# Five seams between stages of a two-layer graph network: barriers and clearing of semaphores taken out, signals for the buffers put in

## The reference

```
xn = layernorm(x)
x  = x + gated graph network(xn, edges) + linear attention(xn)        # layer 0, softmax-like feature map
x  = x + mixture of 8 experts, top 2 (layernorm(x))
xn = layernorm(x)
x  = x + (edge-weighted 1024x1024 matrix applied to xn, + bias) + linear attention(xn)   # layer 1
x  = x + w_down(silu(w_gate xn') * (w_up xn')),  xn' = layernorm(x), integer weights / 127
```

## Time and profile before

| | us |
|---|---|
| median of three runs | 2345.37 |
| lowest and highest | 2345.21, 2346.77 |
| span of the profiled execution | 2343.6 |
| TensorE busy | 2181.0 (93%) |
| VectorE busy | 1513.5 (65%) |
| ScalarE busy | 1015.1 (43%) |
| GpSimd busy | 252.9 (11%) |
| barriers of line 74 | 11 |

### The profile page before, as it was taken

One profiled execution on the slowest core, in us unless ns is written; L12 is line 12 of the kernel. 1 busy time (PEld: TensorE's weight loads), 2 busy tenths in 40 slices (PEclk: granted clock), 3 DMA queues, 4 the chain that ended last, 5 costly groups with the idle time before them and its releaser, 6 DMA issues. The chain is left out here.

```text
span 2343.6 us, 29202 instructions
## 1 busy us (share of the span) xinstructions
PE 2181.0 (93%) x10522; PEld 1799.2 (77%) x10522; DVE 1513.5 (65%) x2245; ACT 1015.1 (43%) x1515; POOL 252.9 (11%) x253
## 2 busy tenths in 40 slices
PE   7999999978968999976999999968999999989998
PEld 4778888867857778775888888856778888878886
DVE  8745474668858788866999999966733333345422
ACT  4134243338725544425888888851022122121120
POOL 0067774000010000020000000011000000000000
PEclk9999999988988999967999999989999999999999
DMA  5431231114448535164555555136420120134224
GB/s 189 143 112 36 50 83 24 65 58 151 146 152 315 215 158 225 46 239 154 182 203 183 209 183 182 63 110 212 133 76 34 48 81 25 63 103 153 75 90 149
DMA packets 114121, 299.89 MB, mean 128 GB/s; under 512 B 18802, under 2 KB 42218, under 8 KB 113974
## 3 DMA queue, kind: packets, MB, share of 16 engines
q1 hardware_dynamic: 103094, 276.52, 33.9%
q0 software_dynamic: 10880, 21.48, 3.3%
HBM read 295.24 MB, written 124.16 MB: 179 GB/s over the span
## 5 line engine op out<-in xcount | busy, mean ns | idle before, releaser
L2717 DVE TENSOR_TENSOR ex_wl<-exlast,ex_wh 128x1024 fp32r<-128x1024 f32 x216 | 252.7, 1220 | 9.1 <-ACT ex_wh L2784 8.5
L2784 ACT ACTIVATE ex_wh<-exlast 128x1024 fp32r<-128x1024 f32 x216 | 217.9, 1059 | 17.3 <-PE ex_pu L2740 8.2
L1267 POOL DMA_INDIRECT scratch_slots<-packed x160 | 196.5, 1228 | 56.7 <-issue 56.7
L324 PE MATMUL ps<-kept,xh 128*128 128x512 f32 (+2 forms) x480 | 160.1, 420 | 7.2 <-DVE xl L3008 5.5
L2117 PE MATMUL gl_bank<-gl_gh,gl_al 125*125 125x512 f32 x385 | 153.5, 399 | 9.7 <-DVE gl_al L2332 9.7
L1564 PE MATMUL ps<-kept,xl 128*128 128x512 f32 (+1 forms) x640 | 159.2, 391 | 0.0
L1566 PE MATMUL ps<-kept,xh 128*128 128x512 f32 (+1 forms) x640 | 158.3, 389 | 0.0
L1570 PE MATMUL ps<-kept,xh 128*128 128x512 f32 (+1 forms) x640 | 158.2, 389 | 0.0
L2119 PE MATMUL gl_bank<-gl_gh,gl_ah 125*125 125x512 f32 x385 | 152.8, 397 | 0.0
L2118 PE MATMUL gl_bank<-gl_gl,gl_ah 125*125 125x512 f32 x385 | 152.6, 396 | 0.0
L1566 PEld LDWEIGHTS ps<-kept,xh 128*128 128x128 f32 (+1 forms) x640 | 118.5, 185 | 26.9
(11 more groups left out here) (513 smaller groups left out, 4885.6 us busy)
## 6 DMA issues: line engine op xcount, KB each, us to landing
exlast<-in_experts SPq DMA_DIRECT2D x216, 512.0 KB
exfirst<-in_experts SPq DMA_DIRECT2D x112, 512.0 KB, 6.2
scratch_seats<-raw SPq DMA_DIRECT2D x95, 512.0 KB
raw<-in_qkv SPq DMA_DIRECT2D x48, 512.0 KB, 5.2
xr<-scratch_res SPq DMA_DIRECT2D x27, 512.0 KB, 4.3
xr<-scratch_seats SPq DMA_DIRECT2D x27, 512.0 KB, 3.7
scratch_res<-xr SPq DMA_DIRECT2D x25, 512.0 KB, 3.9
raw<-in_wo SPq DMA_DIRECT2D x16, 512.0 KB, 4.8
```

Of the source, the lines that this page charges most:

```text
L324: i = e.matmul(o, a, b[:, cut], start=first and n == 0, stop=final and n == 2)
L1267: e.indirect_dma_start(dram["slot_rows"], bass.IndirectOffsetOnAxis(idx[:, k:k + 1].bitcast(U32), 0), pay[:, k, :], None).then_inc(scat.se ...
L2717: return e.tensor_tensor(wl[:, n % RING], raw[unit[1]], wh[:, n % RING].bitcast(F32), ALU.subtract)
L2784: e.activation(wh[:, n % RING], raw[unit[1]], ACT.Copy).then_inc(high.sem)
```

## The change

`Phase` gets a flag `wall`. With `wall=False` (stages `em`, `o0`, `ex`, `se`, `o1`) nothing at all is issued at the stage's end; the semaphores are kept in a common list `spent`. With `wall=True` (`m0`, `gb`, `gl`, `ro`, `m1`, `ff`) a barrier comes first, then the clearing of all of `spent`, then the second barrier. `block()` gives a `Stream` that puts each body straight into the engine's list, without a block of its own and its barrier; only `gb`, which branches, still opens a block (`branches()`), and so keeps the block's barrier too.

The seams without a barrier are `em` to `m0`, `o0` to `gb`, `ex` to `se`, `se` to `m1`, `o1` to `ff`.

```diff
-    def __init__(self, nc, tag):
+    spent = []
+    def __init__(self, nc, tag, wall=True):
...
         if a[0] is None:
-            self.nc.clear_and_free_semaphores(self.sems)
-            self.nc.all_engine_barrier()
+            self.spent += self.sems
+            if self.wall:
+                self.nc.all_engine_barrier()
+                self.nc.clear_and_free_semaphores(self.spent)
+                self.nc.all_engine_barrier()
+                self.spent.clear()
...
     def block(self):
+        return Stream(self.nc)
+
+    def branches(self):
         return self.ctx.enter_context(self.nc.Block())
```

Signals that now guard what is passed on. In `em` and `se` TensorE raises `slot_free` in its last chunk, when a slot of `kept` has been read for the last time, and `attention`'s first four `hi` wait for it; GpSimd in `attention` waits for VectorE's last addition of the stage before (`settled`); TensorE in `ff` waits for the last low part of the normalized input:

```diff
@@ sort_and_embed, TensorE
+                    elif c == TC - 1 and k % 2:
+                        y.then_inc(slot_free.sem)
@@ serve, TensorE
+                    if c == TC - 1 and k < SLOTS:
+                        m.then_inc(slot_free.sem)
@@ attention, GpSimd
         def _(e):
+            e.wait_ge(*settled.last())
             for a in range(2):
@@ attention, ScalarE, hi(u)
                 elif u[0] >= 2:
                     e.wait_ge(*kv_done[u[0] // 2 - 1, TC - 1])
+                else:
+                    e.wait_ge(*slots_free[kv_slot(u)])
                 e.activation(held(0, u), raw[:, nth[u] % SLOTS], ACT.Copy).then_inc(high.sem)
@@ gated_mlp, TensorE
         def _(e):
+            e.wait_ge(*normed_low.last())
```

More of the change, by code:

```diff
@@ L58, in last, with __init__, sync, gpsimd @@
         return self.sem, max(self.value.values())
+class Stream:
+    def __init__(self, nc):
+        self.nc = nc
+    def sync(self, f):
+        f(self.nc.sync)
+    def gpsimd(self, f):
+        f(self.nc.gpsimd)
+    def tensor(self, f):
+        f(self.nc.tensor)
+    def scalar(self, f):
+        f(self.nc.scalar)
+    def vector(self, f):
+        f(self.nc.vector)
 class Phase:
-    def __init__(self, nc, tag):
-        self.nc, self.tag, self.ctx, self.sems = nc, tag, ExitStack(), []
+    spent = []
+    def __init__(self, nc, tag, wall=True):
+        self.nc, self.tag, self.wall, self.ctx, self.sems = nc, tag, wall, ExitStack(), []
     def __enter__(self):
@@ L346, in sort_and_embed @@
     assert all(v * OVER >> SHIFT == v // TP for v in range(N)) and EP < P and EK < 256 and EP < 256 and EK % QC == 0
-    with Phase(nc, "em") as p:
+    with Phase(nc, "em", wall=False) as p:
         sb = p.sb
@@ L379, in sort_and_embed @@
         q_high, q_low, begun = (p.raises(n_, ["q"]) for n_ in ("q_high", "q_low", "begun"))
+        slot_free = p.raises("slot_free", range(3))
         xb, xn = flat(xb), room.take([P, 2, D], F32)
@@ L802, in sort_and_embed @@
         stored = x_out[0:2] + x1_out
-        p.hand_on(*ahead.loaded, *stored, begun)
-    return ahead, stored, begun
+        p.hand_on(*ahead.loaded, *stored, begun, slot_free, done, summed)
+    return ahead, stored, begun, [slot_free[s] for s in range(3)] + [done[TC - 1]], [slot_free, done], summed
 def project(nc, tag, at, xh, xl, w_dram, base, out, raw, first, more, at_stored, base_stored, then, then_scale, xr, kept, ps, ar):
     SLOTS, MADE, BEGUN = 4, 4, 4
-    with Phase(nc, tag) as p:
+    with Phase(nc, tag, wall=False) as p:
         C, U, HALVES = range(TC), range(KC), [slice(0, D // 2), slice(D // 2, D)]
@@ L970, in _ @@
             split(TC - 1)
-        p.hand_on(*ahead.loaded, *x_out, begun)
-    return ahead, x_out, begun
+        p.hand_on(*ahead.loaded, *x_out, begun, low)
+    return ahead, x_out, begun, low
 def project_and_count(nc, tag, at, w_dram, bias_dram, res, dram, c16, first, more, at_stored, xr, halves, ps, ox, ar0):
@@ L1298, in graph_overflow @@
         pw = [ctx.enter_context(nc.psum_tensor(f"gb_pw{i}", [P, 4, P], F32)) for i in range(4)]
-        block = p.block()
+        block = p.branches()
         def some(e):
@@ L1399, in _, with attention @@
                 e.tensor_copy(counted, cacc[:, 0:NBUCK * TP]).then_inc(counts.sem)
-def attention(nc, tag, xh, xl, at, w_dram, bq_dram, bkv_dram, softly, raw, first, then, xr, xr_free, kept, ps, begun, place, onto, beside=None, taken=(), room=None):
+def attention(nc, tag, xh, xl, at, w_dram, bq_dram, bkv_dram, softly, raw, first, then, xr, xr_free, kept, ps, begun, place, onto, slots_free, freed, settled, beside=None, taken=(), room=None):
     PAIRS, SLOTS, RING = KC, 4, 3
@@ L1408, in attention @@
     with Phase(nc, tag) as p:
-        p.take(*first.loaded, *taken, begun)
+        p.take(*first.loaded, *taken, *freed, begun, settled)
         J, C, T = range(PAIRS // 2), range(TC), range(NT)
@@ L2873, in serve @@
         spent, q_high, q_low, begun = (p.raises(n_, ["q"]) for n_ in ("spent", "q_high", "q_low", "begun"))
+        slot_free = p.raises("slot_free", range(SLOTS))
         warm = p.sb("warm", [P, 1])
@@ L3041, in _, with gated_mlp @@
                 evict(c)
-        p.hand_on(*ahead.loaded, *x_out, begun)
-    return ahead, x_out, begun
-def gated_mlp(nc, tag, xh, xl, up_dram, down_dram, hc, dtype, scale, res, out, raw, first, res_stored, xr, kept, ps, begun):
+        p.hand_on(*ahead.loaded, *x_out, begun, slot_free, added)
+    return ahead, x_out, begun, [slot_free[s] for s in range(SLOTS)], [slot_free], added
+def gated_mlp(nc, tag, xh, xl, up_dram, down_dram, hc, dtype, scale, res, out, raw, first, res_stored, xr, kept, ps, begun, normed_low):
     units = 2 * hc
@@ L3053, in gated_mlp @@
     with Phase(nc, tag) as p:
-        p.take(*first.loaded, *res_stored, begun)
+        p.take(*first.loaded, *res_stored, begun, normed_low)
         w = Weights(raw, kept, scale)
@@ L3230, in build @@
                     idx, packed = packed[0:EP, 4].bitcast(I32), flat(packed)
-                    ahead, x_stored, begun = sort_and_embed(nc, xh, xl, io["x"], io["w1"], io["b1"], x1, res, graph, idx,
+                    ahead, x_stored, begun, slots_free, freed, settled = sort_and_embed(nc, xh, xl, io["x"], io["w1"], io["b1"], x1, res, graph, idx,
                                                             pay, spill, raw, io["qkv0"], xr, kept, ps, Room(cnt[:]),
@@ L3235, in build @@
                         nc, "m0", xh, xl, at, io["qkv0"], io["bq0"], io["bkv0"], True, raw, ahead, io["wo0"], xr,
-                        x_stored, kept, ps, begun, place, (ar0[:], ox[:, 0], ox[:, 1], 2),
+                        x_stored, kept, ps, begun, place, (ar0[:], ox[:, 0], ox[:, 1], 2), slots_free, freed, settled,
                         lambda e, p: scatter(e, p, graph, idx, pay, 0, EK), x_stored, Room(cnt[:]))
@@ L3263, in build @@
                 place = [place[:, h] for h in range(2)]
-                ahead, res_stored, begun = serve(nc, "se", xh, xl, served, answer, share, graph["weights"], io["gnn_bias"],
+                ahead, res_stored, begun, slots_free, freed, settled = serve(nc, "se", xh, xl, served, answer, share, graph["weights"], io["gnn_bias"],
                                                  io["bo1"], res, raw, ahead, res_stored, io["qkv1"], xr, served_last, kept, ps,
@@ L3269, in build @@
                                                          ahead, io["wo1"], xr, res_stored, kept, ps, begun, place,
-                                                         (ar[:, 0], xh[:, :, tokens(0)], xl[:, :, tokens(0)], 4))
-                    ahead, res_stored, begun = project(nc, "o1", at, xh, xl, io["wo1"], res, res, raw.bitcast(I32), ahead, more,
+                                                         (ar[:, 0], xh[:, :, tokens(0)], xl[:, :, tokens(0)], 4),
+                                                         slots_free, freed, settled)
+                    ahead, res_stored, begun, normed_low = project(nc, "o1", at, xh, xl, io["wo1"], res, res, raw.bitcast(I32), ahead, more,
                                                        at_stored, res_stored, io["ffn_up"], SCALE, xr, kept, ps, ar)
             gated_mlp(nc, "ff", xh, xl, io["ffn_up"], io["ffn_down"], 3, I32, SCALE, res, io["out"],
-                      raw.bitcast(I32), ahead, res_stored, xr, kept, ps, begun)
+                      raw.bitcast(I32), ahead, res_stored, xr, kept, ps, begun, normed_low)
 def kernel(**a):
```

## The result

| | before | after |
|---|---|---|
| median, us | 2346.07 (6 runs) | 2340.86 (6 runs) |
| lowest to highest | 2345.21 to 2350.25 | 2338.32 to 2342.19 |
| span of the profiled execution | 2343.6 | 2339.2 |
| barriers after clearing | 11 | 6 |
| range clears | 73 | 40 |

The ratio is 0.9968, 95% interval 0.9958 to 0.9977: faster, by 0.23 to 0.42%. The medians of the table differ by 5.2 us (0.22%), just under that interval. I had forecast 14.3 us; the ratio makes it 7.5 of 2346, the two profiled executions 4.4. The new median, 2340.86, lies 0.9 us above the end of my range; beside a kernel before at 2345.4, from which I had worked, the ratio gives 2337.9, inside it. The head of the page answers to the earlier trace rows: the span is shorter and TensorE's busy time the same.

The account below looks back on a forecast made before the run. TensorE, busy 2181 of 2343.6 us, was taken to set the pace in most stages. Terms 4.1 + 2.3 - 0.3 + 1.5 + 3.1 + 2.1 + 1.5 = 14.3 gave span 2329.3, median 2331.1 us; range 2326 to 2340.

Parts of the forecast that it names:

- em to m0, 4.1 us: First seam: TensorE's 1.6 us barrier wait and 2.5 us wait for ScalarE both go; lower end 2.7 us.
- o0 to gb, 2.3 less 0.3: VectorE reaches the end of gb's block 2.3 us earlier; gb's own barriers cost about 0.3 us more.
- ex to se, +1.5 us: Serve's head: ScalarE's earlier start and the gather give 1.5 us, between 0.5 and 2.4.
- se to m1, 3.1 us: Same as the first seam: TensorE's waits of 2.0 and 1.1 us go.
- o1 to ff, 2.1 us: TensorE's barrier wait of 2.1 us goes, as its next group's weights are already in kept.
- The clearing, +1.5 us: At the walls, 33 ranges vanish and about 9 more go, each 0.17 us: 1.5 us gained, bounds -5.6 and +3.
- clearing only moves: Rival: the seams' range clears come back at the walls without merging; gain 7.2 us, time 2338.2; chance 0.12.
- fewer than 40: Sign in the profile after: fewer than 40 range clears are left.
- the 2 us that I had named as a sign of being wrong: Sign at the walls: the prediction is wrong if their clearing takes over 2 us each.
- The slow rival (instruction supply): Rival: without barriers TensorE waits for instructions, 4.0 us at each of five seams; 2351.1, slower; chance 0.06.
- the gains inside attention are lost: Rival: gains in m0 and m1 are lost before their wall; gain 7.1 us, median 2338.3; chance 0.09.
- The change does little: Rival: something just behind the barrier holds each seam; only o1 and gb barrier time saved; about 2347; chance 0.06.

Follow-up runs that it names:

- only_em: Kernel with walls everywhere but at the first seam, em to m0, against the kernel before; ratio 0.9982, span 2339.7.
- ex_wall: Changed kernel with the wall kept at the end of the experts stage (ex) only; ratio to the kernel before 0.9937, 2334.5 us against 2349.1.
- only_ex: Kernel with walls everywhere but at the seam from experts to serve (ex to se), against the kernel before; ratio 1.0024.
- gather_first: Changed kernel, with SyncE in serve waiting for both gathers of chunk 0 before loading weights of units 4 to 7 and rows of chunk 1; ratio 0.9962.
- bias_order: Changed kernel with attention's query bias loaded before the first weights and ScalarE waiting for it after four high parts, not two; ratio to the kernel before 0.9953.
- after_again: The changed kernel itself, unedited, run again beside the kernel before on the follow-ups' chip; ratio 0.9964, span 2337.3.
- after: The changed kernel as first measured against the kernel before; median 2340.86 us, ratio 0.9968, span 2339.2.

## Why the forecast was right in its sign and about twice the measured gain

- **em to m0, 4.1 us: right.** The lead grows by 4.4, and `only_em` has 3.9 us in its span. The bias landed later than I had it (negation at 131.87, not 130.1), which cost nothing: the margin of 1.6 us was there, and no wait is left.
- **o0 to gb, 2.3 less 0.3: right.** `gl` starts 5.5 us behind VectorE's last addition instead of 7.6; the lead grows by 2.2.
- **ex to se, +1.5 us: wrong, it was -5.1.** This is the step that failed. I had the two facts in hand: that the gather can't start before the store lands, and that the DMA engines are 90% busy behind it. I had even written that SyncE's loads now enter ahead of the gathers. I used all this only to shrink the gain, with a lower end of 0.5. What I left out is that an early queue next to one that can't move is harmful: SyncE's loads, which before were held until behind both gathers by ScalarE's late start (`low` of the first weights, itself after the barrier), now pass the second gather. `ex_wall`, `only_ex` and `gather_first` show it from three sides. And the 1.5 was too much even without the collision, where the seam gives 0.4. The Trainium skill states that the queues share the same 16 engines and interleave ("Trainium Kernel Development and Optimization", Key Constraints). These traces agree: the second gather could be used 11.2 us after its issue beside the loads and 5.5 us without them. The consequence here should have been a rival with a negative price, not a smaller gain.
- **se to m1, 3.1 us: 2.2.** The barrier's share came, the bank's wait stayed (1.1, then 1.3), because it hung on the bias's load: issued at 1720.56, negated at 1725.28, 4.7 us later. I had copied the answer of the first seam, where the load is issued 3.3 us before TensorE's first product and not 0.9 (126.68 and 130.00; 1720.56 and 1721.47). `bias_order` takes the wait away.
- **o1 to ff, 2.1 us: right** (2.3).
- **The clearing, +1.5 us: wrong in size.** That the 33 ranges vanish was right (73 became 40, so the rival "clearing only moves" falls). So forty are left, and my sign "fewer than 40" failed: that nine more would go was wrong. Six went, two at `m0`'s wall and four at `m1`'s, and six came, at `gb`, `gl` and `ff`. By the ranges in the two programs the cleared numbers now reach up to 223, and not to 166, with handed-on signals spread among them; that this makes the new gaps is my reading. And I took a range to cost the same whatever its length, while at `m0`'s wall 3 ranges take 1.3 us between the first start and the last (521.7 to 523.0), where 5 took 0.9 (525.9 to 526.8). Of the 1.3 us the long record itself is 0.57; another 0.6 lie between the starts of the second and the third clear, and nothing here explains them. I had expected every wall to gain; 0.9 us of lead went at this one. Added over the six walls, the distance from first to last clear grew from 6.1 us to 7.6: the term was a cost of about 1.5, not a gain of 1.5. The last wall, with 2.1, also passes the 2 us that I had named as a sign of being wrong.
- **The clock.** Not in my sum. The 2.1 us lost early in `o0` and most of the 2.7 in `m1`'s tail stand where TensorE has 1.2 GHz in the one trace and 2.4 in the other. I can't call this an effect of the change: in eleven profiled executions of these kernels the granted clock from 10 to 20 us after `o0`'s first product is between 0.79 and 0.93, and the kernel before happens to hold the highest. With all walls kept it was 0.84. In `after_again`, the same program, `m1`'s tail loses 0.4 us and not 2.7. Over a long stretch a single profile is therefore good to about 2 us and not better. Over the few us of a seam the two profiles of the changed kernel agree within 0.2 us: in `after_again` the five seams read +4.2, +2.2, -5.3, +2.2 and +2.3.

Sum of the leads: +4.4 - 0.9 - 2.1 + 2.2 - 5.1 + 2.2 - 2.7 + 2.3 = 0.3, and what drifts in between: -0.7 in `em`, +1.0 in `m0`, +1.8 in `gl` to the head of `ex`, +1.5 in `se`, +0.5 from `m1`'s tail to `o1`: 4.4 in all, as in the span. Against my sum the five seams alone come to 6.0 (4.4 + 2.2 - 5.1 + 2.2 + 2.3) and the clearing takes up to 1.5 of it; the spans of `after` and `after_again` give 4.4 and 6.3, the ratio 7.5. So one term, of the wrong sign and off by 6.6 us, makes most of the distance from 14.3.

That 2337.9 lies in my range is luck. The range was wide for two rivals, at 2338.2 and 2338.3, and neither happened: the 33 ranges did vanish, and the gains in attention did arrive. A seam that costs time because transfers collide was in no case of mine.

The slow rival (instruction supply) is refuted for TensorE: no wait on "issue" stands at any of the five open seams. So is "the gains inside attention are lost": those of `only_em` arrive. "The change does little", with a seam held by something just behind the barrier, held at one seam of five, and there it was worse than little.

## What to carry to other kernels

Here a barrier also kept order between DMA queues. Before it is taken out, list for every queue what it will issue first, ask which of these transfers the next stage waits for, and whether that one can start earlier at all; if it can't and the others can, make the others wait for it. Where TensorE was busy for 99% of a stage, time saved at the stage's head arrived (4.3 us gained at the first seam alone, 3.9 less in the span). And look at one seam at a time: five edits of one kind held four gains, of 2.2 to 4.4 us, and one loss of 5.1, larger than any of them.

## What the runs showed of the hardware that I had not expected

- A range clear's time grows with its length. The time of each clear stands in the trace, and the numbers that it clears in the built program. The longest clear in all these traces, 567 ns, is the range of 97 numbers at `m0`'s wall, while the shortest ranges take 44 ns; between them lie 304 ns for one of 49 and 200 for one of 32. That is about 5.4 ns for each number ((567 - 44) / 96), and some 0.15 us for each further range with its drain (2.1 us over twelve steps at the end are 0.175 each, of which 0.03 is for their length). By these two figures, and as an estimate, filling a gap pays up to some 25 numbers.
- An indirect gather of 125 rows that shares the DMA engines with plain loads issued around it could be used by VectorE only 11.2 us after its issue (1561.60 to 1572.77). With the loads held back it could be used 5.5 us after its issue (1562.02 to 1567.55).
